# A selective state-space block: the order of VectorE's work inside a step, and the place of one GpSimd multiply in the last steps

## The reference, cut to what matters

```
proj = x @ in_proj_w.T                      # gate, (x, B, C), dt
x, B, C = silu(causal_conv4(...))
dt = softplus(dt + dt_bias);  a = cumsum(-exp(A_log) * dt)   # in chunks of 128 tokens
Y_diag = ((C @ B^T) * exp(a_l - a_s)) @ (x * dt)             # inside a chunk
Y_off  = (C @ state_of_the_chunk_before) * exp(a_l)          # across chunks
y = Y_diag + Y_off + D * x
y = y * rsqrt(mean(y^2) + eps) * norm_w * silu(gate)
out = y @ out_proj_w.T
```

## Time and profile before

| | us |
|---|---|
| median of 3 runs | 1646.56 (1642.46 to 1646.75) |
| the profiled execution's own time | 1649.56 |
| its span | 1647.8 |
| TensorE busy | 1592.1 |
| VectorE busy | 1358.0 |
| ScalarE busy | 1281.6 |
| GpSimd busy | 801.7 |

### The profile page before, as it was taken

The page is one execution under the profiler, slowest core; times in us unless marked ns, Lnnn a source line. Parts: engine busy times, 40 slices in busy tenths (PEclk is TensorE's granted clock), DMA queues, the critical chain, the costliest instruction groups (busy, mean ns, idle before and its releaser), DMA issues.

```text
span 1647.8 us, 27075 instructions
## 1 busy us (share of the span) xinstructions
PE 1592.1 (97%) x8984; PEld 1305.5 (79%) x8984; DVE 1358.0 (82%) x2199; ACT 1281.6 (78%) x2218; POOL 801.7 (49%) x806
## 2 busy tenths in 40 slices
PE   6999999999999999999999999999999999999988
PEld 5888777788888887888788788888788888888766
DVE  5887886888888888887888887898888888878766
ACT  4454459888989798979987898888888888798842
POOL 3565124554556455545554454544554555454460
PEclk9999999999999999999999999999999999999999
DMA  5320345455565446545555455545554645445321
GB/s 174 120 91 1 111 133 155 143 161 148 140 179 153 146 130 176 155 129 150 170 143 160 135 170 143 173 115 172 152 160 131 166 145 160 144 142 161 116 71 52
DMA packets 186074, 229.56 MB, mean 139 GB/s; under 512 B 22384, under 2 KB 122096, under 8 KB 184272
## 3 DMA queue, kind: packets, MB, share of 16 engines
q1 hardware_dynamic: 185936, 227.84, 46.6%
HBM read 190.02 MB, written 37.75 MB: 138 GB/s over the span
## 4 chain that ended last, share of the span: by engine, by line
PE 43%; DVE 20%; issue 9%; ACT 7%; DMA 7%; SPq 1%; POOL 1%; DVEq 0%; ACTq 0%; POOLq 0%
PE bank L160 8%; PE bank L162 7%; PE bank L161 7%; DVE m_xc L1955 7%; PE bank L2343 4%; PE bank L2347 4%; PE bank L2309 4%; PE bank L2344 4%; DMA m_x_rows<-x_turned_rows 4%; DMA x_turned_rows<-m_x_blocks 3%; DVE m_gate L1955 3%; ACT m_mt L1661 2%; DVE m_y L2047 2%; PE bank L2331 2%; DVE xdt L2000 1%
## 5 line engine op out<-in xcount | busy, mean ns | idle before, releaser
L160 PE MATMUL bank<-xh,w_h 128*128 128x512 f32 x1152 | 463.4, 402 | 6.9 <-DVE m_xc L1955 3.9
L162 PE MATMUL bank<-xh,w_l 128*128 128x512 f32 x1152 | 450.9, 391 | 0.0
L161 PE MATMUL bank<-xl,w_h 128*128 128x512 f32 x1152 | 450.5, 391 | 0.0
L1569 POOL TENSOR_TENSOR m_z_l<-m_zg,m_z_h 128x512 fp32r<-128x512 f32 x128 | 179.4, 1401 | 458.2 <-ACT m_z_h L1715 458.2
L1551 POOL TENSOR_TENSOR w_l<-w_raw,w_h 128x512 fp32r<-128x512 f32 x142 | 203.6, 1434 | 228.2 <-ACT w_h L1629 228.2
L1661 ACT ACTIVATE m_mt<-m_mt,m_unit 128x128 f32<-128x128 f32 x1024 | 312.3, 390 | 0.0
L160 PEld LDWEIGHTS bank<-xh,w_h 128*128 128x128 f32 x1152 | 217.1, 188 | 61.9 <-issue 18.9
L162 PEld LDWEIGHTS bank<-xh,w_l 128*128 128x128 f32 x1152 | 216.9, 188 | 46.1
L1955 DVE SCALAR_TENSOR_TENSOR m_xc<-bank,m_par_slots,m_xc 128x1020 f32<-128x1020 f32 (+2 forms) x192 | 243.9, 1270 | 9.9 <-ACT m_xc L1640 5.4
L161 PEld LDWEIGHTS bank<-xl,w_h 128*128 128x128 f32 x1152 | 217.4, 189 | 40.4
L2343 PE MATMUL bank<-m_wo_h,m_z_h 128*128 128x512 f32 x512 | 205.0, 400 | 9.2 <-ACT m_z_h L1715 8.6
(11 more groups left out here) (315 smaller groups left out, 2857.2 us busy)
## 6 DMA issues: line engine op xcount, KB each, us to landing
m_mt<-ncs_rows SPq DMA_DIRECT2D x128, 512.0 KB, 5.8
w_raw<-w_in SPq DMA_DIRECT2D x144, 256.0 KB, 4.2
x_turned_rows<-m_x_blocks SPq DMA_DIRECT2D x120, 256.0 KB, 3.9
m_x_rows<-x_turned_rows SPq DMA_DIRECT2D x480, 64.0 KB, 2.3
m_wo_raw<-w_out_in SPq DMA_DIRECT2D x64, 256.0 KB, 3.9
m_e<-ecs_rows SPq DMA_DIRECT2D x128, 128.0 KB, 3.7
a_wo_raw<-wo_in SPq DMA_DIRECT2D x8, 1024.0 KB, 5.0
x<-x_in SPq DMA_DIRECT2D x8, 256.0 KB, 4.3
```

Of the source, the lines that this page charges most:

```text
L160: nc.tensor.matmul(out, ah, bh, start=first, stop=False)
L161: nc.tensor.matmul(out, ah, bl, start=False, stop=False)
L162: return nc.tensor.matmul(out, al, bh, start=False, stop=last)
L1569: nc.gpsimd.tensor_tensor(z_l[:, s % 2, :, :], zg[:], f(z_h[:, s % 2, :, :]), ALU.subtract).then_inc(zl_ready, 1)
```

## The change

Two edits. On VectorE, in paired steps, `make_y` and `make_z` of tile s-1 come ahead of `add_out(s-2)` and, in even steps, ahead of `times_dt(s)`; the first `turn_blocks` of an odd step stays first. On GpSimd, `to_chunk_end(s)` of the last group's steps 8, 10, 12 and 14 is issued at the end of the step before.

```diff
@@ GpSimd step @@
-                if s % 2 == 0 and own(kind):
+                if s % 2 == 0 and own(kind) and paired(kind, s):
                     to_chunk_end(g, s)
+                if s % 2 == 1 and turned_by_tensor(kind, s):
+                    to_chunk_end(g, s + 1)
@@ VectorE step @@
             def step(g, s, kind):
                 half, t = divmod(s, NT)
+                for made in turned_in(kind, s)[:1]:
+                    turn_blocks(g, made)
+                if paired(kind, s):
+                    for made in made_in(kind, s):
+                        make_y(g, made)
+                        make_z(g, made)
+                if behind(kind, s - 2):
+                    add_out(g, s - 2)
                 for made in scaled_first(kind, s):
                     times_dt(g, made)
-                for made in turned_in(kind, s)[:1]:
-                    turn_blocks(g, made)
-                if behind(kind, s - 2):
-                    add_out(g, s - 2)
...
-                if paired(kind, s):
-                    for made in made_in(kind, s):
-                        make_y(g, made)
-                        make_z(g, made)
                 for made in turned_in(kind, s)[1:]:
                     turn_blocks(g, made)
```

## The result

The changed kernel takes 1652.81 us (median of 9 runs, 1648.68 to 1657.12) against 1643.83 us of the kernel before on the same chip (9 runs, 1640.95 to 1646.95): a ratio of 1.0053, 95% interval 1.0037 to 1.0068. It is slower by 9 us; 1636 was predicted, and the range ended at 1645. The profiled execution has a span of 1652.9 us against 1647.8. That difference of 5.1 us is made up of 18.4 us lost in the groups, 11.3 us won in the late steps, and 2.0 us less in the stretches ahead of and behind these, where nothing was changed: single traces differ by that much on their own (the stretch ahead of the groups took 265.4 to 269.5 us in the fourteen traces).

What follows compares the result with a forecast made beforehand. TensorE, busy 1592.1 of 1647.8 us, was taken as the bound. From the profiled 1649.56 us, 10.5 for late steps and 0 for groups (4.5 - 3.5 - 1.0) gave 1639.1; the median 3.0 lower, 1636 us, range 1629 to 1645.

Steps and rivals of the forecast that it cites:

- Late steps: Last group, steps 9, 11, 13, 15: TensorE's waits before `across` go because xdd comes sooner; 10.5 us won, bounds 7 and 11.5.
- The clock of 0.50 near 1570: Late steps, behind the 3.06 us stand: with no stand TensorE's clock does not fall, 1.65 us won, bounds 0 and 1.65.
- `within`: Step 14: y(13) comes 0.9 us sooner or more, so nearly all TensorE waiting for it goes; 3.5 us won over the groups.
- step 13: In the groups: `taps` come sooner from steps 12 and 10, taking perhaps 1 us of TensorE's z_h waits here.
- Step 4: In the groups: z_h has no slack, so later `taps` cost TensorE 0.2 us; the rest of its wait stays.
- Step 6: In the groups: z_h 0.60 us later against 0.54 us of slack, a new TensorE stand of 0.1 us.
- the late rows: Steps 0, 4, 8: bare row transfer delays VectorE 2.7 us, which falls into the hole before `diag`, 0.6 us cover left.
- the new neighbours: VectorE's z and xdt moved relative to GpSimd's SBUF work: priced at nothing, one gain against one loss.
- The displaced `add_out`: Odd steps: `add_out` now stands behind z, making `turn_blocks` and `taps` 0.60 us later.
- Step 11: In the groups: the same count as step 6, z_h slack 0.5 us, `taps` 0.6 to 1.0 later; 0.3 us lost.
- A: Rival: rows land late in steps 0, 4, 8, TensorE stands 2 us or more a group; 1651 us at bound, chance 0.10.
- D: Rival: GpSimd holds z 1.0 us in each even step, 11 us lost in the groups; 1647 us, chance 0.07.

Runs made afterwards that it cites:

- e1: Only the GpSimd edit made to the kernel before, VectorE in its old order; ratio 0.9923 to the kernel before, median 1632.49 us.
- e3: Both edits, with SyncE issuing the four output-weight loads of step 2 ahead of the read of rows 3; ratio 0.9962 to the kernel before, median 1640.38 us.
- e5: GpSimd edit with VectorE's old order, SyncE holding back the four output-weight loads and four issues behind them; ratio 1.0050 to the kernel before.
- e12: As e3, but odd steps keep the old VectorE order, `add_out` ahead of y and z; ratio 0.9949 to the kernel before.
- e6: As e3, but with the old VectorE order in steps 0, 4 and 8; ratio 0.9878 to the kernel before, median 1629.40 us.
- e10: GpSimd edit and loads of e3, new VectorE order in steps 2, 6, 10, 12 and 14 only; ratio 0.9877 to the kernel before, median 1625.36 us.
- e9: As e3, but GpSimd computes only a sixteenth of `w_low` for the tiles handled in steps 0, 4 and 8; ratio 0.9936 to the kernel before.

## Why the prediction was wrong

- **Late steps: right.** 10.5 us forecast, 11.3 in the trace, e1 shows them alone. The single terms of that sum were not measured one by one. The clock of 0.50 near 1570 is gone with the 3.06 us stand, which e1 and the change both show.
- **`within`: right; step 13: hardly anything there.** The wait of L2397 for y is at most 0.4 us wherever step 14 had the new order, 4.1 us over the groups, 3.5 forecast. Of the 1.0 us of waits for z_h that was to go in step 13, the trace before had 0.3: 5.0 of the 5.3 us between 430 and 1450 us stood in step 4.
- **Step 4 is where the forecast failed.** The text gave it 0.2 us a group: "in step 4, which has no slack at all (part of the 5.3 us), 0.2 us". It measured 1.3 (18.5 - 8.2 us over 8), and with it three stretches at half the clock. The trace before had the chain: z_h of step 4 hangs on `taps` of step 3, and these on the write of x of tile 4. The text followed what the read of rows waits for, and not what stands behind the read on SyncE. There four loads of 256 KB wait in line; they came 2 to 4 us nearer to a transfer that is on the path, and it took 0.5 to 2.3 us longer. e3 takes this away, e5 makes it without the new order. The loads' issue was counted nowhere in the sum.
- **Step 6: the path was seen, its price was not.** The sum had 0.1 us, 0.60 for `add_out` against a slack of 0.54 at z_h, and nothing for the late rows, as 2.7 us of delay fell into a hole with 0.6 us to spare; measured 1.25 a group (10.0 over 8). The 0.6 was worked out from group 3, with a landing of 3.33 us; before, the groups had 3.3 to 4.4 us. The price of the new neighbours was set at nothing: the part across chunks takes 1.64 to 1.66 us beside `w_low` in step 4 and up to 1.83 elsewhere (total 65.9 us in 60, before 41.7), which puts xdt(4) 1 us later, and xdt(5) takes 0.5 to 1.1 us longer. In groups 2 and 6 the landing was the forecast's (3.3 and 3.4 us) and the stand still 0.96 us each; an estimate from these rows, 1.0 + 0.6 us longer less the 0.6 to spare, gives 1.0. The displaced `add_out`, the only term that the sum had, is 0.25 a group here (e12 against e3) and 0.4 where the other causes are gone (e6 against e10).
- **Step 11: nothing came of it** (0.3 us a group forecast). No stand for z_h is there after. The rows of tiles 1 and 9 land as bare as those of tile 5, yet steps 2 and 10 lose nothing. The part across chunks takes 0.7 us there and not 1.64, but no run tests whether that is the reason.
- **Rivals.** A had the right sign and about half of the cause: late rows make the stands of step 6, but those of step 4 come by the write behind the loads, which A does not name. That the total of over 2 us a group (18.4 us in 7.5 groups, 2.5 each) fits its price is in part luck. D's conflict is there, but as a part of the cause (e9). By the Trainium skill ("SBUF — State Buffer", SBUF: two separate sides) a VectorE instruction with two SBUF inputs and a GpSimd one that reads SBUF shut each other out, and the second waits until the first has ended. The trace agrees: the part across chunks takes 1.64 us instead of 0.69 where it starts 0.2 us after a `w_low` of 1.29 us. In place of one gain against one loss the change bought the loss only: z and the part across chunks together took 46 us more VectorE time (123.1 + 65.9 against 101.1 + 41.7), and xdt none less (136.6 against 135.2).

## What to carry to other kernels

When an instruction moves, follow not only what waits for it but what stands behind the waiter in the same queue, DMA issues above all: four weight loads that nobody waited for, 2 to 4 us nearer to the write that counts, brought stands of 10.3 us, nearly what the GpSimd edit won (11.3). Work out a cover from the group with the longest landing, not from the one that is easiest to read, and price a move onto a busy neighbour as well as a move away from one. And a wait on a busy helper engine (39.9 us here) is no gain to be had; the waits of the engine that bounds are (5.3 and 3.1 us).

## What the runs showed of the hardware that was not expected

- A 256 KB write to DRAM behind 1 MB of loads: VectorE went on 2.2 to 2.9 us after its issue in e1, 3.7 to 5.0 us in e5, where the loads had been issued about 5 us ahead of it instead of 8 to 9, and the four smaller issues behind them were later too.
- TensorE's clock fell to 0.50 with stands of 2.0, 2.5 and 2.4 us (by the measure of the table) in step 4 of groups 0, 3 and 4, and not with stands of 2.4 to 2.6 us in groups 1, 2, 6 and 7; after the 3.34 us stand of step 15 of the kernel before it stayed at 1.00 (window 1592.5 to 1599.1 us). The length of a stand alone does not tell whether the clock falls.
